# A two-block shifted-window transformer on one core: the last 32 channels turned several tiles at once

## The reference, cut to what matters

```
x: [8, 16, 56, 56]; DIM = 160, HEADS = 5, WIN = 7, MLP_DIM = 640
sub = conv(relu(x) as [128, 1, 56, 56], f_ana, 9x9)       # 9 channels for each
x3 = concat([sub, relu(x)])  as [8, 56, 56, 160]
for shift in (0, 3):
    h = ln(x3)                            # over the 160 channels
    h = windows of 7x7 of roll(h, -shift)
    q, k, v = split(h @ qkvw + qkvb)
    a = softmax(q @ k.T / sqrt(32) + bias (+ mask if shift))
    x3 = x3 + unroll((a @ v) @ projw + projb)
    x3 = x3 + gelu(ln(x3) @ w1 + b1) @ w2 + b2
x3 = x3 @ linw + linb
y = conv of x3 (f_syn, 9x9), joined with x3, then a 1x1 conv (convw, convb)
```

## Time and profile before

| what | us |
|---|---|
| median of 3 runs | 2950.16 |
| lowest and highest | 2948.86, 2952.37 |
| the profiled execution | 2952.52 |
| its span on the chip | 2951.0 |
| TensorE busy | 2883.9 (98%) |
| VectorE busy | 2213.6 (75%) |
| ScalarE busy | 1721.5 (58%) |
| GpSimd busy | 837.1 (28%) |

### The profile page before, as it was taken

How to read it: one execution, slowest core, us unless ns; L and a number is a source line. 1 busy time by engine, 2 the same in 40 slices (tenths; PEclk the granted TensorE clock), 3 DMA queues, 4 the chain that set the end, 5 groups by cost and what they waited for, 6 DMA issues and landing times. The chain is left out here.

```text
span 2951.0 us, 94022 instructions
## 1 busy us (share of the span) xinstructions
PE 2883.9 (98%) x39898; PEld 2703.9 (92%) x39898; DVE 2213.6 (75%) x6736; ACT 1721.5 (58%) x4076; POOL 837.1 (28%) x1470
## 2 busy tenths in 40 slices
PE   8979999999999999999999999999999999999799
PEld 6669999999999999999999999999999999999799
DVE  5667777887787777787788878778878878887422
ACT  6446666666666666666656655565656555665321
POOL 8122222222222222222323322232323332332111
PEclk9969999999999999999999999999999999999899
DMA  6321111111111111111112221121111111112374
GB/s 155 128 90 25 40 46 43 46 43 46 43 43 30 42 43 46 43 46 43 46 26 47 58 58 34 33 44 44 42 24 44 44 44 25 42 43 46 65 136 77
DMA packets 210768, 152.23 MB, mean 52 GB/s; under 512 B 15954, under 2 KB 205205, under 8 KB 210331
## 3 DMA queue, kind: packets, MB, share of 16 engines
q1 hardware_dynamic: 207619, 142.41, 21.0%
q10 hardware_dynamic: 1008, 3.44, 0.5%
q0 software_dynamic: 1728, 0.48, 0.2%
HBM read 95.64 MB, written 52.50 MB: 50 GB/s over the span
## 5 line engine op out<-in xcount | busy, mean ns | idle before, releaser
L1627 PE MATMUL rm<-w,ht 128*112 128x160 f32 x4480 | 676.5, 300 | 0.0
L1627 PEld LDWEIGHTS rm<-w,ht 128*112 128x112 f32 x4480 | 619.7, 177 | 11.8
L1051 POOL TENSOR_TENSOR rs<-ln_tmp,mhalf 112x4 f32<-112x4 f32 (+1 forms) x128 | 118.8, 928 | 980.3 <-DVE ln_tmp L1233 980.3
L1148 ACT ACTIVATE ht<-rm 128x336 f32<-128x336 f32 (+1 forms) x448 | 216.6, 490 | 124.6 <-PE rm L147 124.5
L1091 ACT ACTIVATE qm<-ra,qpair 128x400 f32<-128x400 f32 x256 | 138.1, 590 | 214.4 <-PE ra L147 214.4
L1124 ACT ACTIVATE pt<-pt_ps 113x490 f32<-113x490 f32 x256 | 149.4, 584 | 184.7 <-PE pt_ps L1566 184.7
L1005 POOL TENSOR_TENSOR z<-z,one 112x448 f32<-112x448 f32 (+2 forms) x192 | 131.4, 684 | 358.2 <-DVE z L1237 358.2
L1119 ACT ACTIVATE pr<-sm 113x490 f32<-113x490 f32 x256 | 159.5, 623 | 88.4 <-DVE sm L1296 87.7
L1338 DVE TENSOR_TENSOR ot_lo<-ra,ot_hi 128x98 fp32r<-128x98 f32 x512 | 109.1, 255 | 128.1 <-ACT ot_rest L1131 118.0
L1131 ACT ACTIVATE ot_hi<-ra 128x98 fp32r<-128x98 f32 x512 | 102.1, 259 | 141.3 <-PE ra L1601 141.3
L1296 DVE TENSOR_TENSOR sm<-sc,mx 113x490 f32<-113x490 f32 x256 | 177.6, 694 | 6.6
(11 more groups left out here) (276 smaller groups left out, 9231.8 us busy)
## 6 DMA issues: line engine op xcount, KB each, us to landing
xa<-xs SPq DMA_DIRECT2D x128, 245.0 KB
xr<-xs SPq DMA_DIRECT2D x128, 245.0 KB
xs<-xo SPq DMA_DIRECT2D x64, 245.0 KB
ys<-yz SPq DMA_DIRECT2D x64, 245.0 KB
c_y<-ys SPq DMA_DIRECT2D x36, 260.0 KB
xs<-a_tok SPq DMA_DIRECT2D x14, 560.0 KB, 6.1
xs<-tok_late SPq DMA_DIRECT2D x14, 560.0 KB, 6.7
a_nat<-in_x ACTq DMA_DIRECT2D x7, 480.0 KB, 6.2
```

The costliest lines, as they stand in the source:

```text
L1148: act_(ht[:, f * SN + t0 * TT:f * SN + (t0 + nt) * TT], bank_m(i, lm, use)[:, 0:nt * TT], ACT.Gelu_apprx_tanh).then_inc(m_freed(i, lm, use ...
L1627: last = mm(bank_m(i, lm, use)[0:TT, t * DIM:(t + 1) * DIM], ht[:, c:c + TT], keep.w["w2", lm][:, f * DIM:(f + 1) * DIM], start=(f == 0), ...
```

## The change

z1, z2 and os lose the repeated columns; z1r and z2r hold the rest channels of all tiles side by side, and GpSimd's rest_apart copies them there. One turn takes four (or three) tiles' rest: tile t lands on PSUM partitions 32 t to 32 t + 31. ScalarE copies each tile's 32 partitions out by itself, VectorE subtracts tile by tile, and the third block is a VectorE copy of the first from SBUF to SBUF. For os the rest of both pairs of windows is turned at once, on partitions 0 to 31 and 32 to 63. The first three passes wait for the low part alone; the rest pass waits on a semaphore of its own. Q0 and K0 put their rest passes last. weights_turned(2) moves behind mlp_out(1).

```diff
-def split_passes(nc, out, hi, lo, rest, w_hi, w_lo, w_rest, act_moves):
+def split_passes(nc, out, hi, lo, rest, w_hi, w_lo, w_rest, act_moves, rest_ready=None, passes=range(4)):
-    for n, (a, w) in enumerate(pairs):
+    for n in passes:
+        a, w = pairs[n]
+        if n == 3 and rest_ready is not None:
+            nc.tensor.wait_ge(*rest_ready)
...
+            def rest_apart(t, r, s, t0=0, nt=ST):
+                gp.tensor_tensor(view(r, 0, TT, t0 * REST, [[REST, nt], [1, REST]]),
+                                 view(t, 0, TT, t0 * DIM + 128, [[DIM, nt], [1, REST]]),
+                                 view(one, 0, TT, 0, [[0, nt], [0, REST]]), ALU.mult).then_inc(s, 1)
...
@@ ScalarE, front_hi (t_hi in the same way)
+                    act.wait_ge(*a_full(i, f"T1C{hf}"))
+                    for t in range(nt):
+                        last = act_(view(z1t[2], 0, REST, (t0 + t) * WIN, [[WP, 16], [1, WIN]]),
+                                    view(bank_a(i, f"T1C{hf}"), t * REST, REST, 0, [[WIN, 16], [1, WIN]]), ACT.Copy)
+                    last.then_inc(s_hi1, 1)
...
@@ VectorE, front_lo (t_lo in the same way)
+                    dve.wait_ge(s_hi1, (i + 1) * 4 + 2 * hf + 2)
+                    for t in range(nt):
+                        ins = v.tensor_tensor(view(z1t[2], REST, REST, (t0 + t) * WIN, dims),
+                                              view(bank_a(i, f"T1C{hf}"), t * REST, REST, 0, [[WIN, 16], [1, WIN]]),
+                                              view(z1t[2], 0, REST, (t0 + t) * WIN, dims).bitcast(F32), ALU.subtract)
+                    ins.then_inc(a_freed(i, f"T1C{hf}")[0], 1)
+                    dims = [[WP, 16], [1, nt * WIN]]
+                    v.tensor_copy(view(z1t[2], 2 * REST, REST, t0 * WIN, dims),
+                                  view(z1t[2], 0, REST, t0 * WIN, dims).bitcast(F32)).then_inc(s_rest1, 1)
...
-                    v.tensor_tensor(view(os_, 0, QP, 128, [[ZW, 2], [HD, 3], [1, HD]]),
-                                    view(so, 0, QP, OC + 4 * VW, [[512, 2], [0, 3], [1, HD]]),
-                                    view(rd, 0, QP, 4, [[HEADS, 2], [0, 3], [0, HD]]), ALU.mult).then_inc(s_od, 1)
+                    v.tensor_tensor(view(os_, 0, QP, 256, [[REST, 2], [1, HD]]),
+                                    view(so, 0, QP, OC + 4 * VW, [[512, 2], [1, HD]]),
+                                    view(rd, 0, QP, 4, [[HEADS, 2], [0, HD]]), ALU.mult).then_inc(s_od, 1)
...
+                def outputs_rest(j):
+                    dims = [[W, 2], [TT, WIN], [1, 2 * WIN]]
+                    v.tensor_copy(view(ot[2], 2 * REST, REST, 2 * j * WIN, dims),
+                                  view(ot[2], 0, REST, 2 * j * WIN, dims).bitcast(F32)).then_inc(s_rest3, 1)
...
@@ TensorE, turn
+                        last = tr(bank_of(use)[0:nt * REST, 0:TT], zr[:, t0 * REST:(t0 + nt) * REST],
+                                  keep.ident[0:TT, 0:TT])
...
@@ TensorE, outputs_turned
+                    last = tr(bank_a(n, use)[0:2 * REST, 2 * QP:3 * QP], os_[:, 256:256 + 2 * REST],
+                              keep.ident[0:QP, 0:QP])
...
@@ TensorE, the body
-                if la is not None:
-                    weights_turned(2, i)
...
                     mlp_out(1)
+                if la is not None:
+                    weights_turned(2, i)
...
-                    front_product("Q", 0)
-                    front_product("K", 0)
+                    front_product("Q", 0, range(3))
+                    front_product("K", 0, range(3))
+                    front_product("Q", 0, range(3, 4))
+                    front_product("K", 0, range(3, 4))
...
-                    pe.wait_ge(*a_freed(i, "OT3"))
+                    pe.wait_ge(s_lo3, NG * (i + 1))
```

More of the change, by code:

```diff
@@ L1080, in front_hi @@
                     t0, nt = HALF[hf]
[L1081 to L1085, removed]
+                    act.wait_ge(*a_full(i, f"T1A{hf}"))
+                    act_(view(z1t[0], 0, 128, t0 * WIN, [[WIN, nt], [WP, 16], [1, WIN]]),
+                         view(bank_a(i, f"T1A{hf}"), 0, 128, 0, [[TT, nt], [WIN, 16], [1, WIN]]), ACT.Copy).then_inc(s_hi1, 1)
+                    act.wait_ge(*a_full(i, f"T1C{hf}"))
[3 more added lines that the diff above has]
+                    last.then_inc(s_hi1, 1)
                 def queries(hf):
@@ L1128, in outputs_hi @@
                     act.wait_ge(*a_full(n, use))
[L1129 to L1132, removed]
+                    dims = [[W, 2], [TT, WIN], [1, WIN]]
+                    for p in range(2):
+                        act_(view(ot[0], 0, 128, (2 * j + p) * WIN, dims),
+                             view(bank_a(n, use), 0, 128, p * QP, [[WP, 2], [WIN, WIN], [1, WIN]]), ACT.Copy)
+                    for p in range(2):
+                        last = act_(view(ot[2], 0, REST, (2 * j + p) * WIN, dims),
+                                    view(bank_a(n, use), p * REST, REST, 2 * QP, [[WP, 2], [WIN, WIN], [1, WIN]]), ACT.Copy)
                     last.then_inc(s_oth, 1)
@@ L1476, in _, with turn @@
             mm, tr = nc.tensor.matmul, nc.tensor.transpose
-            def turn(z, hf, bank_of, room, full, name, freed_already=()):
+            def turn(z, zr, hf, bank_of, room, full, name, freed_already=()):
                 t0, nt = HALF[hf]
-                for part, f0, rows in (("A", 0, 128), ("C", 128, CR)):
+                for part in "AC":
                     use = f"{name}{part}{hf}"
@@ L1483, in turn @@
                         reach(pe, *room(use))
-                    for t in range(nt):
-                        c = (t0 + t) * ZW + f0
-                        last = tr(bank_of(use)[0:rows, t * TT:(t + 1) * TT], z[:, c:c + rows], keep.ident[0:TT, 0:TT])
+                    if part == "A":
+                        for t in range(nt):
+                            c = (t0 + t) * DIM
+                            last = tr(bank_of(use)[:, t * TT:(t + 1) * TT], z[:, c:c + 128], keep.ident[0:TT, 0:TT])
+                    else:
+                        last = tr(bank_of(use)[0:nt * REST, 0:TT], zr[:, t0 * REST:(t0 + nt) * REST],
+                                  keep.ident[0:TT, 0:TT])
                     last.then_inc(full(use), 1)
@@ L1508, in front_turned, with front_product @@
                         pe.wait_ge(s_z[0], i + 2)
[L1509 removed]
+                    turn(z1, z1r, hf, lambda u: bank_a(i, u), lambda u: a_room(i, u), lambda u: a_full(i, u)[0], "T1",
                          ("T1A0",) if steady else ())
[L1512 removed]
+                def front_product(name, hf, passes=range(4)):
                     c0, n = {"Q": (0, 128), "K": (128, 128), "B": (256, 2 * HD)}[name]
                     use = f"{name}{hf}"
[L1515 to L1517 removed]
+                    first = use == "Q0"
+                    if first and 0 in passes:
+                        pe.wait_ge(*a_freed(i, "T1C1" if not steady else "T1A1"))
+                    if 0 in passes and not (first and steady):
                         room_a(use)
[L1519 removed]
+                    last = split_passes(nc, bank_a(i, use)[0:n, 0:QH], *[view(t, 0, t.shape[0], hf * 4 * WP, [[8 * WP, 2], [WP, 4], [1, WQ]])
                                                  for t in z1t],
[L1521 removed]
+                                               *[w[:, c0:c0 + n] for w in keep.w["qkv", ln]], True,
+                                               rest_ready=(s_rest1, 2 * (i + 2)) if first else None, passes=passes)
+                    if 3 in passes:
+                        filled_a(use, last)
                 def values(j, n, l):
```

111 lines of the change are left out of this document (59 added, 52 removed).

## The result

The changed kernel took 2963.68 us (median of 5, 2955.75 to 2969.07) against 2950.16 for the one before: a ratio of 1.0045, with a 95% interval from 1.0027 to 1.0062. It is slower by 13.5 us, where the prediction said 60.

The account below looks back on a forecast made before the run. TensorE was taken to bound the kernel, with VectorE close behind. The terms -0.38, +0.23, +0.35 and +0.76 gave +0.96 us a body, x 62 = 60 us: 3010 us against 2950.16, range 2900 to 3040.

Parts of the forecast that it names:

- S1 on the paths: First turn of z2 to first pass of Q0: VectorE ends it after the change, -0.38 us a body.
- S1, clash of copy and power: VectorE's third-block copy of os group 1 waits until GpSimd's power is over: +0.76 us a body.
- S2: First pass of Q0 to scores(0): Q0's rest pass, behind three K0 passes, delays queries(0), +0.23 us a body.
- S3: scores(0) to the first projection tile's rest pass, which waits for VectorE's third-block copy: +0.35 us a body.
- S4: From the first projection tile's rest pass to the next body: nothing on its path moves, 0.
- the rival B: The paths alone, copies not held by GpSimd: +0.20 us a body, 2962 us; chance 0.22.
- The parts: VectorE's 32 x 112 subtractions, 0.28 us apart: 1.12 for four, 0.84 for three.
- Rival C: Parts and copies at new partitions overlap: -0.92 us a body, 2893 us, or 2907 with held copies; chance 0.28.
- Layer 1: The other kind of body, 30 of 62: given the same sum as layer 0, 0.96 us a body.
- C's floor: In Rival C, TensorE bounds the stretch from z2's first turn to Q0's first pass at 18.00 us.

Follow-up runs that it names:

- e4: The changed kernel with one more GpSimd product of 640 elements into a scratch tile, right behind the power of the z1 chain: 2983.62 us, one run.
- e8: The changed kernel with GpSimd's seven sums x1 + b2 of layer 0 cut to the first: 2953.55 us.
- e11: The changed kernel with one short GpSimd product ahead of layer 0's seven sums, so that they start 0.16 us later: 2957.28 us, one run.
- e2: The changed kernel with the rest pass of Q0 right behind its own three passes, then K0 whole: 2989.11 us.
- e1: The changed kernel without VectorE's eight copies of the third block in a body; the rest passes wait for the subtractions: 2892.11 us.
- e3: The changed kernel with the third block copied by GpSimd instead of VectorE, and the seven sums split into four and three: 2896.63 us.

## Why the prediction was wrong, step by step

| term, us a body | forecast | layer 0 | layer 1 |
|---|---|---|---|
| S1 on the paths | -0.38 | -0.11 | -0.48 |
| S1, clash of copy and power | +0.76 | 0 | 0 |
| S2 | +0.23 | +0.20 | +0.22 |
| S3 | +0.35 | +0.24 | +0.23 |
| S4 | 0 | 0.00 | +0.01 |
| sum | +0.96 | +0.33 | -0.02 |

**The step that failed is the clash**: "the cast of os group 1 is due at 2.52, inside the power, and would wait until 3.29: +0.76". It was due where the prediction said, 1016.68 against a z1t_rest that starts at 1014.11, inside a power of 1.49, and took 0.25. I had carried the one row of a held copy from a run of 20 streaming products to a single instruction of 7 elements, by their lengths. Without this term the sum is +0.20, or 2962 us: the rival B, which I had given 0.22. The measured 2963.68 is 1.7 from it, but that closeness is partly luck: the bodies gave +0.32 in one layer and nothing in the other, +0.16 on average, where B has +0.20 in both. The page "SBUF — State Buffer" of the Trainium skill, section "Who interferes with whom", on which that sentence leaned, has the two sides take the ports in turn for an instruction's whole length. With e4's product the trace agrees (the copy of 0.33 ends 0.18 behind it, so all but 0.15 of it comes after); with the power it doesn't (0.25 inside it), and the measurement decides.

**S1's engine was right, its size wasn't.** VectorE ends S1, without a wait but the 0.31 for ScalarE's four copies (0.39 forecast), and Q0 starts 0.05 behind it. The stretch is 19.04, not 18.77. The term left out is GpSimd's other work: VectorE's path, longer by the new parts, slid so that sm, which reads two inputs from SBUF, met one of the seven sums (the third, by the estimate above) and took 0.98 for 0.67. e8 without the sums has 18.78. The kernel before had sm beside the same sums and escaped the price by the moment at which it began (e11). A hint stood in its layer 1, which I hadn't read: sm takes 0.89 there. The path also had a fourth wait, the 0.17 ahead of the first z2t_lo in the earlier trace rows, which the sum passed over; its end moved the path by 0.04 only.

**The parts were sized rightly.** Four parts took 1.12 and three 0.83 (forecast 1.12 and 0.84), ScalarE's four 1.04 to 1.07, copies 0.39, 0.33 and 0.25. Rival C, overlapping parts, is out. The page "VectorE: DVE Perf Modes" of the Trainium skill, section "Two Vector instructions with no wait between them", says that parts at other partitions start only when those before are finished; 0.28 apart at 0.27 each agrees.

**S2** came out within 0.03, and e2 shows that the wait which the order hides is real (0.39 of idle time). **S3** was +0.24 for +0.35: VectorE's chain to the copy's end grew from 8.12 to 8.72 behind scores(0), 0.60 where I had summed 0.71. **S4** held.

**Layer 1** was given layer 0's sum without being read. Its S1 gained 0.48, so that the whole change is nothing there. The same additions on layer 1's own rows, in which VectorE waited only 0.43, 1.42 and 0.47 us for ScalarE and 0.55 for TensorE, would have given 21.60, or -0.30. Measured is 0.18 less. Of it 0.16 is sm, which ran beside GpSimd's product before the change already (0.89) and takes 0.73 after; the copy of z2's second half takes 0.14 of that back (0.47 for 0.33). The other 0.16 is spread over small joints, as in layer 0.

**C's floor was wrong too.** It let TensorE bound S1 at 18.00 once VectorE is short. e1 and e3 stop at 18.30, on ScalarE in e3. That C's times of 2893 and 2907 lie around e3's 2896.6 all the same is chance: in e3 the copies are off VectorE, which C hadn't supposed, S3 gave 0.15 where C had nothing, and S2 cost 0.12 where C had 0.23.

## What to carry to other kernels

When a change moves work from the engine that bounds to the one right behind it, look for what the moved work needs at the earliest and who is idle then: the third block needed only ScalarE's copy, and GpSimd did it for nothing, where on VectorE it cost 1.28 us a body. Before you carry a contention from one row to another place, compare what the other engine's instruction is and how much it moves, not only how long it lasts, and look at all of that engine's instructions along the path, not only at one. And read each kind of body by itself: the same diff was worth +0.32 in one layer and nothing in the other.
